# A decoder layer on one core: TensorE takes over three of GpSimd's eight additions per batch, and five steps change their place

## The reference

```python
q = (h @ Wq)...   # h = layernorm(x); 32 heads of 64
k = (h @ Wk)...; v = (h @ Wv)...           # 8 groups, each shared by 4 heads
q = rope(q); k = rope(k)
scores = (q k^T + alibi) / 8
scores = 30 * tanh(scores / 30)
scores = where(causal, scores, -inf)
probs = softmax(scores)                    # over the keys
x = x + (probs @ v).reshape(...) @ Wo + bo
...
x = x + xattn(ctx, ctx, layernorm(x))      # a long convolution per head, by Toeplitz products
x = x + ffn(layernorm(x))                  # gated, with ternary weights: each group of 64 weights is
                                           # rounded to -1, 0 or 1 times its mean magnitude
```

## Time and profile before

| | value |
|---|---|
| median of three executions | 1192.57 us |
| the profiled execution, its own time | 1189.52 us |
| its span, first to last instruction | 1187.8 us |
| TensorE matmuls busy | 1135.1 us, 96% |
| VectorE busy | 873.6 us, 74% |
| GpSimd busy | 688.1 us, 58% |
| ScalarE busy | 550.9 us, 46% |
| mean granted TensorE clock | 0.995 of full speed |
| `add_keys`, L1996 | 56 times, 1633 ns each |

### The profile page before, as it was taken

The page is one execution under the profiler, slowest core; times in us unless marked ns, Lnnn a source line. Parts: engine busy times, 40 slices in busy tenths (PEclk is TensorE's granted clock), DMA queues, the critical chain, the costliest instruction groups (busy, mean ns, idle before and its releaser), DMA issues.

```text
span 1187.8 us, 27043 instructions
## 1 busy us (share of the span) xinstructions
PE 1135.1 (96%) x10867; PEld 809.3 (68%) x10882; DVE 873.6 (74%) x1287; ACT 550.9 (46%) x617; POOL 688.1 (58%) x557
## 2 busy tenths in 40 slices
PE   4988999999999999999999899999999999999998
PEld 4665567656667666576676577777886876786683
DVE  6879787877877868778788688888745644654654
ACT  6766564655646646646466400000244543542441
POOL 0454394784865947948759589999343422423331
PEclk9998999999999999999999999999999999999999
DMA  9463335454345344553454457773001122013000
GB/s 323 150 198 122 121 101 157 138 177 145 108 161 174 99 147 152 150 161 113 152 174 140 161 110 143 145 145 87 1 19 41 15 54 54 14 39 54 19 19 36
DMA packets 166183, 134.15 MB, mean 113 GB/s; under 512 B 69628, under 2 KB 127362, under 8 KB 166082
## 3 DMA queue, kind: packets, MB, share of 16 engines
q1 hardware_dynamic: 141128, 126.44, 36.5%
q10 hardware_dynamic: 24960, 6.29, 3.6%
HBM read 81.76 MB, written 35.21 MB: 98 GB/s over the span
## 4 chain that ended last, share of the span: by engine, by line
PE 61%; issue 11%; POOL 9%; DVE 8%; DMA 6%; ACT 3%; SPq 1%; POOLq 0%; DVEq 0%; ACTq 0%
PE bank L962 13%; PE bank L1040 9%; PE bank L1041 9%; PE bank L700 6%; PE bank L701 6%; PE bank L702 6%; PE bank L1059 5%; POOL region_c L1987 4%; PE bank L1058 4%; DMA wffn<-w_p 3%; POOL parts L1982 2%; PE bank L788 1%; POOL key_sum L1996 1%; DMA unit_halves<-halves 1%; DVE wffn L1591 1%
## 5 line engine op out<-in xcount | busy, mean ns | idle before, releaser
L1982 POOL TENSOR_TENSOR parts<-parts 128x512 f32<-128x512 f32 x80 | 131.8, 1649 | 119.1 <-DVE parts L1445 119.1
L700 PE MATMUL bank<-hT_halves,w_hi 128*128 128x256 f16 x640 | 177.0, 276 | 4.8 <-DVE hT_halves L1429 4.1
L701 PE MATMUL bank<-hT_halves,w_hi 128*128 128x256 f16 x640 | 176.6, 276 | 0.0
L702 PE MATMUL bank<-hT_halves,w_lo 128*128 128x256 f16 x640 | 176.6, 276 | 0.0
L962 PE MATMUL bank<-kv,toep 128*128 128x288 f32 (+2 forms) x660 | 157.8, 401 | 0.7 <-ACT qT L1210 0.5
L962 PEld LDWEIGHTS bank<-kv,toep 128*128 128x128 f32 x660 | 123.7, 190 | 34.0 <-ACT qT L1210 0.8
L1987 POOL TENSOR_SCALAR_AFFINE_SELECT region_c<-region_c 128x512 f32<-128x512 f32 x128 | 109.0, 874 | 52.7 <-ACT region_c L1176 52.7
L2130 POOL TENSOR_TENSOR sqsum<-sqsum,toep 128x512 f32<-128x512 f32 x56 | 77.2, 1379 | 95.7 <-ACT toep L1352 95.6
L2000 POOL TENSOR_TENSOR ctx_lo<-ctx,ctx_hi 128x512 f16<-128x512 f32 x64 | 89.0, 1394 | 61.7 <-ACT ctx_hi L1152 61.6
L1158 ACT CAST halves<-parts 128x512 f16<-128x512 f32 x80 | 49.3, 616 | 137.4 <-POOL parts L1982 135.3
L1040 PE MATMUL bank<-odd_halves,guT 128*128 128x256 f16 x512 | 112.2, 273 | 0.0
(11 more groups left out here) (192 smaller groups left out, 2628.2 us busy)
## 6 DMA issues: line engine op xcount, KB each, us to landing
unit_halves<-halves SPq DMA_DIRECT2D x80, 256.0 KB, 2.2
q_both<-unit_halves SPq DMA_DIRECT2D x64, 256.0 KB, 2.9
q_high<-unit_halves SPq DMA_DIRECT2D x64, 128.0 KB, 3.0
toep<-kernel_padded SPq DMA_DIRECT2D x32, 256.0 KB, 4.1
wffn<-w_gu SPq DMA_DIRECT2D x6, 1280.0 KB, 6.7
cpair<-ctx_pairs SPq DMA_DIRECT2D x32, 176.0 KB, 4.9
xin<-x SPq DMA_DIRECT2D x8, 512.0 KB, 9.7
region_o<-wq SPq DMA_DIRECT2D x4, 1024.0 KB, 11.5
```

The source lines that it names most:

```text
L700: pe.matmul(dst, lh, rh, start=first and k == 0, stop=False)
L701: pe.matmul(dst, lh, rl, start=False, stop=False)
L702: mm = pe.matmul(dst, ll, rh, start=False, stop=last and k == n - 1)
L1982: pool.tensor_tensor(slot[:, 0], slot[:, 0], slot[:, 1], ALU.add).then_inc(unit_summed, 1)
```

## The change

`ADDED` names the groups whose key tiles GpSimd still adds: 0, 4, 5, 6, 7. In groups 1, 2 and 3 of batches 1 to 7 TensorE sums both tiles with `weigh`, as in the first batch. The buffers of `key_sum` and the semaphore counts follow the position in `ADDED`. Beside that:

- `find_above(b)` goes from step 0 of batch b + 1 to the early units of batch b, behind the rotation of early unit 4 (for batch 0: to the end of `first_batch`, which is the same place in time).
- The statistics of x2 go from step 1 to step 7, behind those of the next input, which stay in step 1. `deviation` on GpSimd goes from step 5 to step 1, `keep_x2` from step 5 to step 8, and SyncE's load of the residual waits for the later statistics.
- `round_share` goes from step 8 to step 9, behind `ctx_hi` of group 6.

```diff
+ADDED = (0, 4, 5, 6, 7)
 # SyncE
-                next_residual(b, 4 * TT * b + 2 * TT)
+                next_residual(b, 4 * TT * b + 4 * TT)
 # TensorE, values()
-                if first:
-                    if g:
-                        pe.wait_ge(rsum_turned, g)
+                if first or g not in ADDED:
+                    if NG * b + g:
+                        pe.wait_ge(rsum_turned, NG * b + g)
                     weigh(bank[:, SUM_BANK, 0:S], g % 3, lambda t: sum_ones[:]).then_inc(sums_filled, 1)
                     return
-                pe.wait_ge(keys_added, NG * (b - 1) + g + 1)
+                pe.wait_ge(keys_added, len(ADDED) * (b - 1) + ADDED.index(g) + 1)
 # ScalarE, attend()
-                    if step == NG:
+                    if step == NG + 1:
                         round_share(b)
 # VectorE, attend()
                     if step == 0:
-                        find_above(b - 1)
                         find_below(b - 1)
                     if step == 1:
+                        prepare(b + 1, 2 * TT * b)
+                    if step == 7:
                         for i in range(TT):
-                            statistics_of_x2(i, 2 * TT * b)
-                        prepare(b + 1, 2 * TT * b + TT)
+                            statistics_of_x2(i, 2 * TT * b + TT)
...
                     if n == 0:
                         find_thresholds(b)
+                    if n == 4:
+                        find_above(b)
                     if n:
                         low_unit(b + 1, n - 1)
 # GpSimd, attend() and last_batch()
-                    if 1 <= step < NG + 1:
+                    if step - 1 in ADDED:
                         add_keys(b, step - 1)
 # GpSimd, attend()
-                    if step == 5:
-                        keep_x2(b - 1, 4 * TT * b + 2 * TT)
-                        deviation(b + 1, 4 * TT * b + 4 * TT)
+                    if step == 1:
+                        deviation(b + 1, 4 * TT * b + 2 * TT)
+                    if step == NG:
+                        keep_x2(b - 1, 4 * TT * b + 4 * TT)
```

More of the change, by code:

```diff
@@ L628, in _ @@
             next_share(B - 2)
-            next_residual(B - 2, 4 * TT * (B - 2) + 2 * TT)
+            next_residual(B - 2, 4 * TT * (B - 1))
             place_early(B - 1)
@@ L814, in values @@
                 for j in range(REP):
-                    mm = pe.matmul(bank[j * SQ:(j + 1) * SQ, SUM_BANK, P:S], sum_ones[:], key_sum[:, g % 2, j, :], start=True, stop=True)
+                    mm = pe.matmul(bank[j * SQ:(j + 1) * SQ, SUM_BANK, P:S], sum_ones[:], key_sum[:, ADDED.index(g) % 2, j, :], start=True, stop=True)
                 mm.then_inc(sums_filled, 1)
@@ L1760, in first_batch @@
                 low_unit(1, EARLY - 1)
+                find_above(0)
             first_batch()
@@ L1993, in add_keys @@
                 pool.wait_ge(masked, n)
-                if g >= 2:
-                    pool.wait_ge(sums_filled, n - 2)
-                pool.tensor_tensor(key_sum[:, g % 2], sc_first[:, g % 3, :, P:S], sc_second[:, g % 3], ALU.add).then_inc(keys_added, 1)
+                if ADDED.index(g) >= 2:
+                    pool.wait_ge(sums_filled, NG * b + ADDED[ADDED.index(g) - 2] + 1)
+                pool.tensor_tensor(key_sum[:, ADDED.index(g) % 2], sc_first[:, g % 3, :, P:S], sc_second[:, g % 3], ALU.add).then_inc(keys_added, 1)
             def low_ctx(b, g):
```

## The result

| | before | after |
|---|---|---|
| median, same chip | 1192.06 us (5 executions, 1188.61 to 1193.26) | 1178.10 us (5 executions, 1176.09 to 1184.07) |
| the profiled execution, own time | 1189.52 us | 1184.07 us |
| its span | 1187.8 us | 1182.3 us |

The ratio is 0.990, 95% interval 0.9875 to 0.9925: faster by about 12 us. It is not the ratio of the medians, which is 0.9883. The profiled execution after was the longest of its five.

A forecast was written before the change was run, and what follows sets the result against it. TensorE was taken to set the pace, so removing its pauses pays: gains 20.3 + 2.0 = 22.3 us, losses 4.5 + 7.4 + 0.2 = 12.1, net -10.2, median 1182.4 us. Likeliest 1180 to 1186; range 1176 to 1190.

The forecast's parts named there:

- The count of sums: Key sums of groups 1 to 3 on TensorE: 21 groups more, 0.21 us each, a certain loss of 4.5 us.
- The removed pauses: TensorE's recurring waits, 21.4 us with 0.16 us correction each, go except 1.1 us in the last batch: gain 20.3 us.
- The five kinds: TensorE waits for a rotation, `key_sum`, turned sums, group 3's tanh and `ctx_lo`: 17.4 us in 25 pauses.
- The transition: `find_above` among the early units delays unit 6 and the next batch's first tanh: 1.3 us, six times, net 7.4 us lost.
- a shorter hold: Pending GpSimd work delays `low_unit` 3 by 0.31 us instead of 1.07; transition loss then about 0.7, elsewhere 0.6.
- The costs put at nothing: `deviation` in step 1, x2's statistics in step 7 and `round_share` a step later were each forecast to cost nothing.
- The cover named in the prediction: Group 1's causal zeros, behind `deviation`'s wait, are due about 0.6 us later than they come; without it, up to 1 us.
- The end of the last batch: Unit 9 lands earlier, x2's load and 1/std about 2.5 us earlier, transposes wait less: gain 2.0 us, bounds 0 and 3.3.
- rival 1: The transition costs little, about 0.6 us each, `low_unit` 3 losing 0.31 us or less: median 1178.1 us; chance 0.25.
- Rival 2: Group 0 keeps its wait, its zeros or addition overlapping VectorE's last pass: 5.5 us kept, 1187.9 us; chance 0.13.
- Rival 3: Slower: `find_above` is paid nearly in full at each transition, 4.2 us each, 1199.7 us; chance 0.08.
- Rival 4: No change: half the removed waits return at other links of the same chain, 1193.5 us; chance 0.06.

The follow-up runs named there:

- Kernel 12: Kernel 8 with all eight groups' key tiles summed on TensorE in every batch; median 1177.61 us, ratio 0.9900, batch 77.86 us.
- kernel 5: The changed kernel run again unaltered, against the kernel before; median 1179.48 us, ratio 0.9893, batch 77.92 us.
- kernel 9: The changed kernel with `find_above` back in step 0 and `deviation` back in step 5; median 1179.38 us, ratio 0.9912, batch 77.89 us.
- Kernel 2: Steps only: the changed kernel, but GpSimd adds the key tiles of all eight groups; median 1186.18 us, ratio 0.9965, batch 79.03 us.
- kernel 1: Sums only: the kernel before with groups 1, 2 and 3 summed on TensorE, no step moved; median 1184.42 us, ratio 0.9943, batch 78.92 us.
- kernel 3: The changed kernel with `find_above` back in step 0; median 1182.80 us, ratio 0.9935, batch 78.57 us.
- kernel 10: Kernel 8 with `deviation` put back in step 1; median 1180.81 us, ratio 0.9923, batch 78.58 us.
- kernel 4: The changed kernel with `find_above` behind early rotation 3 instead of 4; median 1184.48 us, ratio 0.9940, batch 78.68 us.
- kernel 7: The changed kernel with the last batch's first `scale_digits` moved from step 1 to behind step 2's rotation; median 1179.67 us, ratio 0.9890.
- kernel 11: Kernel 8 with the last batch's first `scale_digits` moved behind step 2's rotation; median 1172.86 us, ratio 0.9857, batch 77.01 us.
- kernel 8: Kernel 9 with group 0 also summed on TensorE, GpSimd adding groups 4 to 7 only; median 1174.71 us, ratio 0.9851, batch 77.01 us.
- kernel 6: The changed kernel with `round_share` back in step 8; median 1181.43 us, ratio 0.9905, batch 77.98 us.

## Why the prediction was right, and where it wasn't

**The count of sums** is right. By the groups of matmuls by form, after:

```profile
L814 PE MATMUL bank<-region_c,sum_ones x280: 272/273/297, 146.7 to 662.0; 128*32 128x128 f32 x140
...
L789 PE MATMUL bank<-region_c,sum_ones x232: 379/379/403, 55.2 to 634.1; 128*32 128x256 f32 x116
```

L789 has 232 records at 8 a group, 29 groups, of which 8 are the first batch's: 21 more. Kernel 12 gives the price, 0.21 us, and so a floor: 77.01 with four groups on GpSimd, 76.80 with five, 76.16 with eight. Batch 1 bears it out. In kernel 5 nothing is waited for there, and it takes

```profile
135.48:212.28 76.80, 76.80 (x937) 51.79 (x936) 64.24 (x96) 43.39 (x40) 48.13 (x40) 1.00 0.41 123
```

In the kernel before it takes 76.92, with one wait of 0.6 us: 76.16 + 0.6 + 0.16. The batch before is 79.78, 3.62 above its floor; after, 77.92 (kernel 5), 1.12 above. Every batch time minus its floor is what waits cost in it.

**The removed pauses**: forecast 20.3 us. The five kinds fell from 17.4 us in 25 to 1.6 in 2, that is 15.8, with 23 x 0.16 us of correction 19.5. The correction is borne out by kernel 9: 76.80 + 5.6 / 6 + 0.16 = 77.89, to the digit. It is no general constant: at the transition's waits of kernel 5 (2.8 and 4.0 us, six times each) 0.47 + 0.67 = 1.13 needs none. The pause of `key_sum` left in the last batch is there, at 1.0. But the reason given for one of them failed: "the rotation of unit 9 comes 3 us earlier, by these and by the three additions saved". Kernel 2 has the first without the second and keeps the 6.6 us; kernel 1 the reverse, and loses them. The turned sums, too, did not need `find_above` gone from step 0, as the prediction had it: kernel 9 has it there and no such wait.

**The transition**: forecast 1.3 us each, 7.4 net; 1.12 in the batch time, and by the view 4.2 + 2.7 - 0.4 = 6.5 in all. `low_unit` 3 took 1.76 us, the value for "right". The Trainium skill (SBUF — State Buffer, § Who interferes with whom) has the pair of ports held for a whole instruction by whoever issues first; this row agrees. VectorE's L1580 in the earlier trace rows, 1.40 us for 1.09 with GpSimd's zeros pending, remains a shorter hold than the rule's. Two things in the step were off: the loss shows at two places, 0.4 us at the scores and 0.7 at `v_s`, not 1.2 at `v_s` alone, and the slot that `high_unit` 6 waits for was not in it. The loss by the shorter hold is given as 0.7 us in one place of the prediction and 0.6 in another; 1.3 less 1.07 - 0.31 is 0.6.

**The costs put at nothing.** `deviation` in step 1: nothing in the change, since in its three passes the statistics come 0.20 us late only; kernels 3 and 10 show 0.68 and 1.57 us a batch once `find_above` stands ahead of them again. The cover named in the prediction was real and thin, and its bound of 1 us was too small. `round_share`: nothing but one wait of 0.9 us, not visible in the time. The statistics of x2 in step 7: no wait came. They are more than free: kernel 9 differs from kernel 1 by them (with `keep_x2`, the residual load and `round_share`, which move nothing that TensorE waited for in kernel 1's three batches), and is 78.92 - 77.89 = 1.03 us a batch shorter. That is as much as all the steps together gain on kernel 1 (78.92 - 77.92). No run moves the statistics alone, so that they are what did it is argued, from the waits of kernel 1 that are gone: the turned sums behind them and the tanh of group 3.

**The end of the last batch**: forecast 2.0 us, measured 1.4. In kernel 5 the whole last batch is 1.35 us shorter. The rotation gives 1.73, the sums take 0.64, and the transition, which lies within this stretch too, takes about 1.1: 1.35 - 1.73 + 0.64 + 1.1 = 1.4 is left for the end. It is seen at the transposes, before and then in kernel 5:

```profile
658.11 0.66 PE L859 MATMUL bank<-ident_s,hbuf 128*128 128x128 f32 x4 [0.69 <-DVE hbuf L1647]
659.40 0.66 PE L859 MATMUL bank<-ident_s,hbuf 128*128 128x128 f32 x4 [0.64 <-DVE hbuf L1647]
```

```profile
649.37 2.02 PE L860 MATMUL bank<-ident_s,hbuf 128*128 128x128 f32 x12
```

Counted from the start of the batch, `hbuf` comes 1.0 us earlier (44.4 us against 45.4) and not 2.5; both waits go all the same.

**The sum.** With the terms as measured 19.5 + 1.4 - 4.5 - 6.5 = 9.9 us, where 10.2 was forecast. From the start of the values' projection of batch 1 to the convolution kernel 5 takes 536.84 us and the kernel before 546.78: 9.9 less. So the mechanism held, and the sum with it. The whole span of kernel 5 is only 8.7 us shorter, since it reaches batch 1 1.3 us later, within the spread of that stretch. In the frame of profiled executions the forecast was 1179.3 us, kernel 5's own time is 1180.84.

The medians moved by 12 to 14 us. They lie below the 1180 to 1186 that the forecast held likeliest, at 0.42, and inside its range; that the first is 1178.1, rival 1's time to the digit, is luck and does not speak for rival 1: its mark, a `low_unit` of 0.7 us, is absent. What was mis-sized is the step from profiled executions to medians. The one before was short (1189.52; its medians are 1190.56 to 1192.57), both of after were the longest of theirs. Part of it goes with the clock. In the 36 executions of the kernel before beside kernels 1 to 12, a mean granted clock lower by 0.001 goes with 1.0 us more (a straight line through them, correlation -0.76). They average 0.9939, the eleven of the changed kernel 0.9958, which makes an estimated 1.9 us of the 12 to 14. Why the changed kernel has the higher clock, no run shows; the rest stays open.

Rival 2 is out in the change (`key_sum` waits once) and true in kernels 3 and 9. Rival 3's price is out. Rival 4's time is out; its mechanism, that a removed wait comes back one link further on, is what happened in kernels 3, 4, 7 and 10.

## What to carry to other kernels

Fix the floor first: vary the one cost that is certain (here the number of groups summed on TensorE) until a stretch shows the engine busy for its whole length, and then every variant's distance from that floor is its waits, to 0.1 us, where medians blur by 2. Count what stands between the profiled execution and the median apart from the change. Moving a long pass on VectorE that GpSimd stood still for only moved the collision; what paid was to take away the work that stood behind it (group 0's addition, 0.21 us on the bottleneck for 1.09 of waiting). And a short instruction that waits at the head of its engine's list costs what is behind it, not what it does: a `deviation` that starts with 0.22 us of work cost 1.57.

## What the runs showed of the hardware

TensorE's clock falls in some executions and not in others of the same code. Windows of the kernel after, in the last batch and in the convolution:

```profile
650.00:655.00 5.00, 2.70 (x55) 1.80 (x54) 4.90 (x9) 1.55 (x4) 2.17 (x2) 1.00 1.06 397
655.00:660.00 5.00, 4.88 (x18) 2.25 (x19) 3.24 (x7) 3.30 (x9) 1.49 (x2) 0.66 0.53 177
...
825.00:830.00 5.00, 4.42 (x31) 3.81 (x30) 4.56 (x11) 0.00 (x0) 1.59 (x1) 1.00 0.00 0
830.00:835.00 5.00, 5.00 (x19) 4.16 (x19) 3.32 (x7) 0.62 (x1) 3.11 (x3) 0.66 0.00 0
```

In the first place TensorE had waited; its timeline then shows the half level, 1.2 GHz, products 0.43 us apart where they are 0.22 elsewhere:

```profile
654.97 1.50 PE L860 MATMUL bank<-ident_s,hbuf 128*128 128x128 f32 x8 [2.19 <-ACT qT L1211]
656.27 0.63 PE L701 MATMUL bank<-region_o,ctx_hi 128*128 128x512 f16 x1
656.70 0.63 PE L702 MATMUL bank<-region_o,ctx_hi 128*128 128x512 f16 x1
```

In kernel 5 neither fall happens, though the stretch before the second has the same 4.42 us of busy time in 5:

```profile
825.00:830.00 5.00, 4.42 (x30) 3.69 (x30) 4.81 (x13) 0.62 (x1) 0.93 (x1) 1.00 0.00 0
```

From the last batch's end to the next phase the convolution takes 162.83 us in executions without the fall (kernels 5, 9, 11, 12) and 164.19 in kernel 8: 1.36 us for one fall. Kernels 1 and 10 show the fall in the convolution too, at 1.35 us, and kernel 6 at 1.0; kernel 3 shows the one in the last batch. The kernel after had both, and that is part of its 1182.3 against 1179.1: its last batch took 72.28 us against kernel 5's 69.22. When the clock falls and when not was not settled.
